# Sparse graph attention on one core: ScalarE weighs some gathered rows, VectorE adds pairs of rows, and the rounds of ScalarE and TensorE are written in another order

## The reference

```python
Wh = h @ W                                   # per head
e = leaky_relu(f_src[:, None] + f_dst[None, :], 0.2)
attn = softmax(where(adj > 0, e, -9e15))     # per head
h_prime = attn @ Wh                          # layer 2 then applies elu
```

## Time and profile before

| | |
|---|---|
| median of the runs | 1292.91 us |
| profiled execution | 1299.03 us |
| its span, first to last instruction | 1295.5 us |
| layer 1, first gather to the last product of the mean | 576 to 829 us |
| layer 2, first gather to the store of its end | 832 to 1069 us |
| TensorE matmul busy in the span | 925.6 us (71%) |
| VectorE busy | 910.5 us (70%) |
| ScalarE busy | 393.7 us (30%) |
| GpSimd busy | 688.7 us (53%) |
| mean granted TensorE clock | 0.866 |

### The profile page before, as it was taken

One profiled execution on the slowest core, in us unless ns is written; L12 is line 12 of the kernel. 1 busy time (PEld: TensorE's weight loads), 2 busy tenths in 40 slices (PEclk: granted clock), 3 DMA queues, 4 the chain that ended last, 5 costly groups with the idle time before them and its releaser, 6 DMA issues.

```text
span 1295.5 us, 12201 instructions
## 1 busy us (share of the span) xinstructions
PE 925.6 (71%) x2854; PEld 500.2 (39%) x2854; DVE 910.5 (70%) x2785; ACT 393.7 (30%) x1174; POOL 688.7 (53%) x645
## 2 busy tenths in 40 slices
PE   3988899894037477756999999667877761756774
PEld 2333344341025355543556555323444340322332
DVE  4888879992168598836878877177888972747663
ACT  3544566451023133321322323224334440101010
POOL 4043331307577777617777600277776005777773
PEclk9988999898568789987999999877878875978888
DMA  9979887651477688726667610266676015656662
GB/s 362 347 253 345 306 295 275 235 170 46 129 229 241 189 258 261 242 88 183 191 169 207 194 50 34 75 175 179 186 214 195 36 48 133 174 144 174 188 180 94
DMA packets 81445, 242.72 MB, mean 187 GB/s; under 512 B 16932, under 2 KB 19396, under 8 KB 77276
## 3 DMA queue, kind: packets, MB, share of 16 engines
q0 software_dynamic: 47488, 144.09, 39.1%
q1 hardware_dynamic: 33882, 97.82, 20.8%
HBM read 203.00 MB, written 53.64 MB: 198 GB/s over the span
## 4 chain that ended last, share of the span: by engine, by line
PE 27%; DVE 23%; POOL 19%; issue 13%; DMA 12%; ACT 4%; POOLq 1%; SPq 0%; ACTq 0%
POOL arena L1064 13%; PE psum L666 9%; PE psum L689 8%; DVE arena L1357 4%; PE psum L625 4%; DVE arena L1298 3%; DMA arena<-XV,arena 3%; DMA arena<-T,arena 3%; ACT arena L781 2%; DMA arena<-in_L_gnn_a 2%; PE psum L584 2%; DVE arena L1180 2%; DVE arena L1113 2%; DVE arena L1267 2%; POOL LIST L1049 2%
## 5 line engine op out<-in xcount | busy, mean ns | idle before, releaser
L1064 POOL DMA_INDIRECT arena<-T,arena x476 | 514.0, 1080 | 353.3 <-issue 167.4
L689 PE MATMUL psum<-arena,misc 128*128 128x512 f32 x476 | 258.0, 668 | 63.3 <-DVE arena L1357 63.3
L666 PE MATMUL psum<-arena 128*128 128x264 f32 (+1 forms) x832 | 224.9, 416 | 47.2 <-ACT arena L781 47.2
L603 PE MATMUL psum<-misc,arena 128*128 128x128 f32 (+1 forms) x520 | 87.2, 294 | 181.8 <-ACT arena L765 114.6
L625 PE MATMUL psum<-arena 128*128 128x512 f32 (+1 forms) x416 | 200.5, 625 | 20.6 <-ACT arena L794 11.7
L666 PEld LDWEIGHTS psum<-arena 128*128 128x128 f32 (+1 forms) x832 | 164.9, 203 | 126.3 <-ACT arena L781 72.8
L765 ACT ACTIVATE arena<-arena 128x512 f32<-128x512 f32 x104 | 84.9, 817 | 275.5 <-DVE arena L1274 255.4
L1357 DVE TENSOR_TENSOR arena<-arena 128x512 f32<-128x512 f32 x238 | 161.8, 688 | 1.8
L689 PEld LDWEIGHTS psum<-arena,misc 128*128 128x128 f32 x476 | 96.6, 214 | 154.8 <-issue 122.8
L603 PEld LDWEIGHTS psum<-misc,arena 128*128 128x128 f32 (+1 forms) x520 | 65.0, 150 | 233.2 <-ACT arena L765 124.9
L735 PE MATMUL psum<-arena 128*128 128x512 f32 (+1 forms) x208 | 112.8, 692 | 17.9 <-ACT arena L778 17.9
(11 more groups left out here) (137 smaller groups left out, 1053.1 us busy)
## 6 DMA issues: line engine op xcount, KB each, us to landing
arena<-in_adj SPq DMA_DIRECT2D x25, 1663.5 KB, 9.2
T<-arena SPq DMA_DIRECT2D x75, 260.0 KB, 3.6
arena<-T,arena POOLq DMA_INDIRECT x476, 3.8
T<-arena SPq DMA_DIRECT2D x25, 256.0 KB, 3.1
XV<-arena SPq DMA_DIRECT2D x25, 256.0 KB, 3.9
PW<-arena POOLq DMA_DIRECT2D x5, 1024.0 KB, 9.3
arena<-in_x SPq DMA_DIRECT2D x1, 3072.0 KB, 16.2
XV<-arena SPq DMA_DIRECT2D x1, 3072.0 KB, 18.9
```

What stands on the lines that cost most here:

```text
L603: last = e.transpose(p_t[:, k * P:k * P + n], src[0:n, k * P:(k + 1) * P], ident[0:n, 0:n])
L666: last = e.matmul(p_wh[0:n, a, :], ht[:, k, 0:n], WL[l][:, k, a, :], start=k == 0, stop=k == 3)
L689: e.matmul(p_num[s % 3].rearrange("p (a o) -> p a o", a=2), ident, halves(GB[:, BASE[l, s] + k, :])[:, :, 0:HALF], start=k == 0, stop=k == ...
L1064: e.indirect_dma_start(GB[:, BASE[l, s] + k, 0:ROW], None, dr["T"][l], bass.IndirectOffsetOnAxis(ap=(IDP if l else IDX)[:, t, k:k + 1], ax ...
```

## The change

In layers 1 and 2, the last `BY_ACT` rows of a tile are weighed by ScalarE instead of VectorE, with one ACTIVATE (copy with a scale from SBUF) for each head. In layer 1, the first `2 * PAIRS` rows are weighed by VectorE and added in pairs, so that TensorE sums one row for a pair. Per attention layer 35 rows go to ScalarE, and layer 1 has 25 pairs. The order of the work in a round changes as well: ScalarE takes `exp` of tile r, not r-1, near the end of round r; in layer 1 `node_ht` and `products_out` come a round later; TensorE turns a tile at the end of the round in layer 1 and after the second sum in layer 2; `products` of a tile comes a round later and starts beside the third sum. The buffer of `new_h` is doubled, and the ring has 31 rows instead of 32.

```diff
-NS = 32
+NS = 31
+BY_ACT = {1: 0, 2: 0, 3: 1, 4: 1, 5: 2, 6: 2, 7: 2, 8: 2, 15: 5}
+PAIRS = {1: 0, 2: 0, 3: 0, 4: 1, 5: 1, 6: 2, 7: 2, 8: 2, 15: 4}
+def units(l, t):
+    n, act = SLOTS[t], BY_ACT[SLOTS[t]]
+    pairs = PAIRS[n] if l == 1 else 0
+    return [(2 * k, "pair") for k in range(pairs)] + [(k, "one") for k in range(2 * pairs, n - act)] + [(k, "act") for k in range(n - act, n)]
...
-    H = take(D)
+    HB = [take(D) for _ in range(2)]
...
-            for r in range(1, NT + 4):
-                if 0 <= r - 4 < NT:
-                    node_tr(ORDER[r - 4], (l + 1) * NT + r - 4, None if l == 1 else WO[(r - 4) % 2])
-                n = SLOTS[ORDER[r - 1]] if r - 1 < NT else 0
-                for k in range(max(n, 4)):
+            for r in range(1, NT + 5):
+                n = len(units(l, ORDER[r - 1])) if r - 1 < NT else 0
+                turned = 0 <= r - 4 < NT
+                for k in range(max(n, 6)):
                     if k < n:
                         sums(l, r - 1, k)
-                    if l == 1 and k < 4 and 0 <= r - 4 < NT:
-                        products(l, r - 4, k)
-                if l == 2 and 0 <= r - 4 < NT:
+                    if l == 1 and 2 <= k < 6 and 0 <= r - 5 < NT:
+                        products(l, r - 5, k - 2)
+                    if l == 2 and k == 1 and turned:
+                        node_tr(ORDER[r - 4], 3 * NT + r - 4, WO[(r - 4) % 2])
+                if l == 1 and turned:
+                    node_tr(ORDER[r - 4], 2 * NT + r - 4)
+                if l == 2 and turned:
                     scores_of(r - 4)
...
+        def weigh(l, s):
+            NH, F = HEADS[l], D // HEADS[l]
+            j, n = (l - 1) * NT + s, SLOTS[ORDER[s]]
+            for k, kind in units(l, ORDER[s]):
+                if kind == "act":
+                    row = halves(GB[:, BASE[l, s] + k, :])
+                    e.wait_ge(S["normalized"], j + 1)
+                    for h in range(NH):
+                        a, b = divmod(h * F, HALF)
+                        part = row[:, a, b:b + F]
+                        last = e.activation(part, part, ACT.Copy, scale=E[j % 2][:, k * NH + h:k * NH + h + 1])
+                    last.then_inc(S["scaled"], 1)
...
-            for r in range(1, NT + 6):
-                if r - 1 < NT:
-                    exp(l, r - 1)
+            out = 6 if l == 1 else 5
+            for r in range(NT + out):
                 if l == 2 and 0 <= r - 2 < NT:
                     elu(r - 2)
-                if 0 <= r - 5 < NT:
-                    if l == 1:
-                        products_out(l, r - 5)
-                    else:
-                        scores_out(r - 5)
-                if 0 <= r - 4 < NT:
-                    node_ht(ORDER[r - 4], (l + 1) * NT + r - 4)
+                if l == 1 and 0 <= r - 6 < NT:
+                    products_out(l, r - 6)
+                if l == 2 and 0 <= r - 5 < NT:
+                    scores_out(r - 5)
+                if 0 <= r + 1 - out < NT:
+                    node_ht(ORDER[r + 1 - out], (l + 1) * NT + r + 1 - out)
+                if 0 <= r - 1 < NT:
+                    weigh(l, r - 1)
+                if r < NT:
+                    exp(l, r)
                 if 0 <= r - 3 < NT:
                     new_h(l, r - 3)
...
+            for k, kind in units(l, ORDER[s]):
+                if kind == "one":
+                    weighed(k).then_inc(S["weighed"], 1)
+                    yield
+                if kind == "pair":
+                    pair(weighed(k))
+                    yield
+                    pair(weighed(k + 1))
+                    yield
+                    pair.wait()
+                    e.tensor_tensor(row(k), row(k), row(k + 1), ALU.add).then_inc(S["weighed"], 1)
+                    yield
```

More of the change, by code:

```diff
@@ L36, with count @@
 FIRST = [sum(SLOTS[t] for t in ORDER[:s]) for s in range(NT + 1)]
-NS = 32
+NS = 31
[5 more added lines that the diff above has]
+    return [(2 * k, "pair") for k in range(pairs)] + [(k, "one") for k in range(2 * pairs, n - act)] + [(k, "act") for k in range(n - act, n)]
+def count(l, s, kinds):
+    ahead = [(i, t) for i in range(1, l + 1) for t in (ORDER if i < l else ORDER[:s])]
+    return sum(kind in kinds for i, t in ahead for _, kind in units(i, t))
+ALL, BY_DVE = ("pair", "one", "act"), ("pair", "one")
 class Signals(dict):
@@ L443, in wait_used @@
         elif l < 3:
-            e.wait_ge(S["summed"], (l - 1) * TOTAL + n)
+            e.wait_ge(S["summed"], count(l, s, ALL) + max(i for i, (first, _) in enumerate(units(l, ORDER[s])) if first <= k) + 1)
         else:
@@ L687, in sums @@
                     wait_num_read(e, *(divmod(i - 3, NT) if s >= 3 else (l - 1, NT - 1)))
-            e.wait_ge(S["weighed"], (l - 1) * TOTAL + FIRST[s] + k + 1)
+            kinds = ("act",) if kind == "act" else BY_DVE
+            e.wait_ge(S["scaled" if kind == "act" else "weighed"], count(l, s, kinds) + sum(kd in kinds for _, kd in of[:n + 1]))
             e.matmul(p_num[s % 3].rearrange("p (a o) -> p a o", a=2), ident, halves(GB[:, BASE[l, s] + k, :])[:, :, 0:HALF],
-                     start=k == 0, stop=k == SLOTS[ORDER[s]] - 1).then_inc(S["summed"], 1)
+                     start=n == 0, stop=n == len(of) - 1).then_inc(S["summed"], 1)
         def mean(l):
@@ L859, in new_h @@
                 wait_row_free(l, s)
-            node_h(WO[s % 2] if l == 2 else H, ORDER[s], m, small[m % 2][:, 8:9], small[m % 2][:, 9:10])
+            node_h(WO[s % 2] if l == 2 else HB[m % 2], ORDER[s], m, small[m % 2][:, 8:9], small[m % 2][:, 9:10])
         def elu(s):
-            e.wait_ge(S["summed"], TOTAL + FIRST[s + 1])
+            e.wait_ge(S["summed"], count(2, s + 1, ALL))
             if s >= 2:
@@ L1323, in shifted @@
                 e.wait_ge(S["blended"], FIRST[s - 1])
+            if l < 3 and s >= 2 and BY_ACT[SLOTS[ORDER[s - 2]]]:
+                e.wait_ge(S["scaled"], count(l, s - 1, ("act",)))
             soft(e.tensor_tensor(u, d, SM[:, l % 2, t, 0:NH].unsqueeze(1).broadcast_to([P, n, NH]), ALU.add))
@@ L1350, in normalized, with weigh, row, weighed @@
             yield
-        def weigh(l, s, k):
+        pair = Steps(e, S["pair_step"])
+        def weigh(l, s):
             j, n, NH, u = weights_of(l, s)
[L1354 to L1357, removed]
+            def row(k):
+                return halves(GB[:, BASE[l, s] + k, :])[:, :, 0:HALF]
+            def weighed(k):
+                both = row(k).rearrange("p a (h o) -> p a h o", o=D // NH)
+                p = u[:, k, :].rearrange("p (a h) -> p a h", a=2).unsqueeze(3).broadcast_to([P, 2, NH // 2, D // NH])
+                e.wait_ge(S["normalized"], j + 1)
+                return e.tensor_tensor(both, both, p, ALU.mult)
+            for k, kind in units(l, ORDER[s]):
[10 more added lines that the diff above has]
+                    yield
         def finish(l, s):
             x, num = X[:, ORDER[s], :], p_num[s % 3]
-            e.wait_ge(S["summed"], (l - 1) * TOTAL + FIRST[s + 1])
+            e.wait_ge(S["summed"], count(l, s + 1, ALL))
             if l == 1:
@@ L1386, in vector @@
                 go(nz)
-                for k in range(SLOTS[ORDER[r - 1]] if on else 0):
-                    weigh(l, r - 1, k)
+                for k, _ in enumerate(weigh(l, r - 1) if on else none):
                     go(nrm, 2)
```

17 lines of the change are left out of this document (9 added, 8 removed).

## The result

The changed kernel takes 1322.66 us (median of four runs, 1320.73 to 1324.56), against 1296.79 for four runs of the kernel before on the same chip. The ratio is 1.020, with a 95% interval of 1.0166 to 1.0235: slower by 2%. The forecast was 1299, slower by 0.5%, which is less than a measurement of this kernel tells from no change. The measured time lies 2 us under the upper end of the stated range (1325). The profiled execution took 1324.56, its span is 1322.8 against 1295.5.

A forecast was written before the change was run, and what follows sets the result against it. TensorE was taken to bound layer 1, no engine to fill layer 2, where the exponent waited behind a store. 2.3 + 5.2 - 9 + 8.6 = +7 on the profiled 1299; on the median 1292.9, 1299 us; range 1245 to 1325.

The forecast's parts named there:

- rival A: Layer 2: TensorE's clock falls once in each pair of rounds, twelve rounds by 2.16 us; +24, 1317 us; chance 24%.
- the clock term: Layer 2: half clock costs 2.16 us in each round behind the four tiles of 2 rows, +8.6 us.
- the ring: Layer 2: VectorE's rows, two sums, transposes, node_ht, exponent wait in a circle; 6.2 us plus 1.17 per ScalarE row.
- the wait for ScalarE: Layer 1: TensorE waits 1.65 us for ScalarE's row ahead of the third sum; 22 rounds take 191.6 against 189.3, +2.3.
- full clock: Layer 1: TensorE stays at full clock, also with 1.65 us idle in rounds of 8.3.
- The end of layer 1: Behind layer 1's last sum, three rounds of 5.63 us become four: 22.1 for 16.9, +5.2.
- the store: Layer 2: the exponent no longer waits for the store (4 us behind scores_out); new_h does, late in the round.
- the -9 of the prediction: Layer 2, second tile to last, before the clock term: 191.3 us against 199.8.
- The price of a ScalarE row: Eight 64-column ACTIVATEs of 0.237 us, 1.89 a row in layer 1; four of 0.29, 1.17 in layer 2.
- Rivals B and C: B: ScalarE's ACTIVATEs don't overlap, 1331 us, chance 10%. C: ScalarE's rows come cheap, 1263 us, chance 18%.
- Rival D: Both layers: rings do not bind, only the work; layer 1 gains 21.5 us; kernel 1227; chance 12%.

The follow-up runs named there:

- the kernel with fillings: Changed kernel plus constant multiplications into an unused PSUM bank in layer 2 and one TensorE wait ahead of it: 1301.93 us, ratio 1.0058.
- the best kernel: Changed kernel with ScalarE rows in layer 2 alone and TensorE's transposes first in its layer 2 rounds: 1259.83 us, ratio 0.9714.

## Why the prediction was right about the direction and short in size, point by point

The forecast was +7 us on the profiled execution and the measured difference is +27.3. The direction was as forecast. That the time still lies in the range is owed to rival A (1317), which the range took in.

**The step that failed is the clock term, +8.6: the rounds that it counts.** It had four rounds at half clock, those behind the tiles of two rows, because "a ScalarE row's sum breaks the empty stretch in most rounds". The times from one exponent's reader to the next, over all of layer 2, show it otherwise. The rounds out of tiles of three and four rows take 7.43 to 7.47 (predicted 7.37), apart from the one behind the 15 rows, and those out of the third and fourth of the tiles of two rows take 6.28 (6.2): no half clock on the ring there. The ten rounds out of tiles of five rows and more, without the very first, are longer than the ring by 1.48 to 2.44 us, together by 19.6. That is rival A, nearly once in each pair; it had twelve rounds at 2.16, 26 us. Layer 2's stretch is 210.9, which is 191.3 + 19.6; that the sum closes so well is in part luck, since the round out of the first tile of eight rows took 3.3 us less than the ring and those out of the second tile of two rows and the tile of three behind the 15 rows took 1.8 and 2.2 more. In the kernel with fillings nine of these ten rounds are within 0.2 us of the ring and the first is 1.0 above it, so the clock is what they had lost to. The sum of ScalarE's row breaks no empty stretch, because it is what TensorE waits for: the row comes 2.39 us late, and the two sums behind it are slow too.

The evidence for rival A lay in the earlier trace rows, where the clock fell once in a pair, and I let an argument speak against it that had no row behind it. The mean clock of the stretch gave no warning: it is 0.87, above the 0.83 of before.

**Layer 1, the wait for ScalarE: right; "full clock": wrong in the two longest rounds.** TensorE waits 1.53 us (1.65 predicted), and rounds are 8.37 and 9.38 us (8.3 and 9.2). The round of seven rows took 12.15 for 10.5 and that of 15 rows 18.10 for 16.4. In both TensorE waits for VectorE's adding instruction, 1.90 us in the first and 1.54 and 0.90 in the second, and that is about the wait that the prediction's sums leave for it (2.2 and 2.9). What it did not have is what comes behind the wait (changed kernel, TensorE, and the granted clock of two stretches):

```profile
628.27 3.45 PE L711 MATMUL psum<-arena,misc 128*128 128x512 f32 x4 [1.90 <-DVE arena L1420]
631.52 1.32 PE L685 MATMUL psum<-arena 128*128 128x264 f32 x4
665.97 1.90 PE L711 MATMUL psum<-arena,misc 128*128 128x512 f32 x2 [0.90 <-DVE arena L1420]
667.66 1.97 PE L685 MATMUL psum<-arena 128*128 128x264 f32 x4
...
628.20:631.50 3.30, 3.23 (x4) 1.31 (x5) 2.02 (x7) 3.23 (x13) 2.39 (x4) 0.57 0.55 163
667.60:669.40 1.80, 1.80 (x5) 1.35 (x4) 1.80 (x4) 1.80 (x10) 1.50 (x2) 0.50 0.70 171
```

Two sums take 3.45 us where they take 1.88 elsewhere, one sum 1.90 for 1.13, two products 1.97 for 1.05. That is half clock, and it makes 3.3 of the 5.4 us by which 197.0 exceeds 191.6. The run without ScalarE rows has the same waits in its round of 15 rows (1.49 and 0.90) and no half clock behind them, and the round takes 16.55 (in its round of seven rows the half clock shows again):

```profile
662.58 1.13 PE L711 MATMUL psum<-arena,misc 128*128 128x512 f32 x2 [0.90 <-DVE arena L1420]
```

The rest of the 5.4 is 0.1 to 0.2 a round.

**The end of layer 1: right.** Four rounds of 5.63 us, 22.08 in all for 22.1, at full clock: +5.2.

**Layer 2, the store: right.** Moving the exponent ahead of it alone gains 15.3 us in the kernel before. It shows that the -9 of the prediction was a net of this gain and of the ring, which I had worked out as one number.

**The price of a ScalarE row: right.** Eight ACTIVATEs a row, 3.93 us for two rows where the estimate was 3.78; in layer 2, 1.28 and 2.44 for 1.17 and 2.34. Rivals B and C fall with it.

**Rival D falls in the changed kernel**: VectorE lost 20 us of work in layer 2 and the layer grew by 12. The Trainium skill (Perfetto Trace Analysis, "Optimizing Scalar/DVE Operations") says that offloading work to ScalarE may make sense where VectorE is saturated. The trace does not bear it out for this order of work; it does with the transposes first, for 7.7 us.

In numbers: layer 1 +12.9 (7.7 in the rounds, 5.2 at the end) for the predicted +7.5, layer 2 +11.1 for +0.1 (-8.5 before rounding, and the 8.6). Of the 16.4 us between them the half clock makes 14.3 (11.0 in layer 2, where it is 19.6 for 8.6, and 3.3 in layer 1). What remains unassigned is 0.4 us in layer 1 and 1.3 us in layer 2 between the stretches and their stages, and the +1.8 of layer 3, which is no more than two executions of unchanged stages differ.

**What stays open**: whether anything is to be had from the waits that are left in layer 2 of the best kernel, the 29.2 us for gathers above all, since no run moved them. It is also open why the clock fell in some rounds and not in others with the same idle time. Nor was it tried whether pairs that VectorE adds earlier would give the rest of the 21.5 us in layer 1.

## What to carry to other kernels

Before work is moved to an idle engine, write down the ring that its new place closes: who it waits for in the round, and who waits for its result in the same round. Here the same 35 rows on ScalarE cost 22 us with TensorE's transposes behind two sums and gained 8 with the transposes ahead of them. A low clock cost time here only where instructions that others waited for were slow: look at their durations, not at the mean, which stood at 0.82 both in the changed kernel's layer 2 (256.7 us) and in the fastest one (221.1).

## What the runs showed of the hardware

- In the changed kernel's layer 1 TensorE stayed at 2.4 GHz with 1.53 us of idle time in each round of 8.37, and in its end with 1.36 in each 5.63. In the two long rounds it fell to 1.2 GHz behind 1.90 us of idle time, and behind 1.54 and 0.90 with one sum between them.
- In layer 2 instructions ran at 1.2 GHz behind an idle time of 2.39 us that had four transposes ahead of it. The same 2.39 us were also followed by a sum at full speed (1.13 us at 968.06), and there the slow ones began behind the next idle time, of 0.78 us (two sums in 3.75 at 970.76). Two fillings of 448 columns (1.67 us) behind the transposes and one behind the scores raised the layer's clock from 0.82 to 0.91, and shortened it though they are added work.
- An ACTIVATE with a scale from SBUF, in place, takes 0.245 us for 64 columns (3.93 / 16) and 0.29 for 128 ((2.44 - 1.28) / 4) back to back, close to the estimate from 32-column copies (0.237 and 0.29).
